# Four heads' shift rows transposed together at the end of the preceding unit, window values produced token-major, and two reorderings on VectorE, in a sparse attention and expert kernel

## What is computed

```python
s_b   = einsum('bhtd,bhnd->bhtn', q, k_c) / scale          # 32 compressed blocks of 16 tokens
out_c = softmax(where(c_ok, s_b, NEG)) @ v_c
_, top_idx = top_k(logits_c, 4)                            # four blocks per token
out_s = softmax over the 64 tokens of the chosen blocks    # selected branch
out_l = softmax over the last 33 tokens                    # window branch
out   = (g0 * out_c + g1 * out_s + g2 * out_l) @ Wo
```

## Time and profile before

| | |
|---|---|
| median of 3 runs | 1492.84 us |
| the profiled execution: its time, its span | 1490.08 us, 1488.3 us |
| busy: PE, DVE, ACT, POOL | 1399.5, 1148.8, 927.1, 946.8 us |
| mean DMA traffic | 76 GB/s |

### The profile page before, as it was taken

How to read it: one execution, slowest core, us unless ns; L and a number is a source line. 1 busy time by engine, 2 the same in 40 slices (tenths; PEclk the granted TensorE clock), 3 DMA queues, 4 the chain that set the end, 5 groups by cost and what they waited for, 6 DMA issues and landing times. The chain is left out here.

```text
span 1488.3 us, 43616 instructions
## 1 busy us (share of the span) xinstructions
PE 1399.5 (94%) x14864; PEld 1041.1 (70%) x14960; DVE 1148.8 (77%) x4512; ACT 927.1 (62%) x1684; POOL 946.8 (64%) x877
## 2 busy tenths in 40 slices
PE   6899569999999999999999999999999999999978
PEld 4566437777777777777777777777777777777757
DVE  5444378888888888888888888888888888888712
ACT  3776436666666666666666666666666666666641
POOL 4655357777777766666666666666676666666720
PEclk8999969999999999999999999999999999999989
DMA  6556842211112222222212222122222222222027
GB/s 187 202 192 213 269 82 54 52 44 48 46 47 51 52 52 52 52 50 47 47 47 47 50 52 47 48 52 52 52 52 52 52 52 52 66 52 53 9 83 250
DMA packets 217149, 113.76 MB, mean 76 GB/s; under 512 B 128872, under 2 KB 211224, under 8 KB 217112
## 3 DMA queue, kind: packets, MB, share of 16 engines
q1 hardware_dynamic: 216304, 112.88, 27.9%
q10 hardware_dynamic: 808, 0.42, 0.2%
HBM read 73.08 MB, written 40.16 MB: 76 GB/s over the span
## 5 line engine op out<-in xcount | busy, mean ns | idle before, releaser
L1394 DVE TENSOR_REDUCE bmax<-q_bank 128x32 f32<-128x512 f32 (+3 forms) x512 | 221.2, 487 | 34.4 <-PE q_bank L1635 34.2
L1149 POOL TENSOR_TENSOR sumxy<-xy 128x1024 f32<-128x1024 f32 x128 | 246.1, 1942 | 0.0
L1241 ACT ACTIVATE pts<-k_bank 128x512 f32<-128x512 f32 (+2 forms) x384 | 177.4, 490 | 42.2 <-PE k_bank L1670 41.4
L1115 POOL TENSOR_TENSOR pad<-pad 128x1 f32<-128x1 f32 x32 | 6.2, 193 | 287.4 <-DVE top L1413 287.4
L1495 DVE SCALAR_TENSOR_TENSOR mw<-sumxy,c,ex 128x1024 f32<-128x1024 f32 x128 | 162.0, 1287 | 13.4 <-ACT ex L1259 9.6
L1617 PE MATMUL f_bank<-xt,wfu 128*128 128x128 f32 x1024 | 162.4, 281 | 0.0
L1635 PE MATMUL q_bank<-ko,qo 96*128 96x512 bf16 (+3 forms) x512 | 142.6, 306 | 16.9 <-DVE bmax L1394 16.7
L1175 POOL TENSOR_TENSOR cw<-cw,mw 128x1024 f32<-128x1024 f32 x64 | 150.9, 2358 | 11.5 <-ACT mw L1265 8.9
L1617 PE MATMUL f_bank<-xt,wfg 128*128 128x128 f32 x1024 | 150.3, 279 | 0.0
L1617 PEld LDWEIGHTS f_bank<-xt,wfu 128*128 128x128 f32 x1024 | 139.4, 191 | 11.5
L1318 ACT ACTIVATE oT<-k_bank 128x512 f32<-128x512 f32 x64 | 38.2, 597 | 173.8 <-PE k_bank L1685 129.3
(11 more groups left out here) (211 smaller groups left out, 3307.8 us busy)
## 6 DMA issues: line engine op xcount, KB each, us to landing
qo<-s_qs SPq DMA_DIRECT2D x192, 64.0 KB, 2.2
ko<-s_ks SPq DMA_DIRECT2D x186, 64.0 KB, 2.2
s_qs<-parts SPq DMA_DIRECT2D x8, 768.0 KB, 4.7
s_ks<-parts SPq DMA_DIRECT2D x8, 768.0 KB, 6.3
s_v<-vo SPq DMA_DIRECT2D x8, 544.0 KB, 3.0
vv<-s_v SPq DMA_DIRECT2D x32, 136.0 KB, 2.3
vw<-s_v SPq DMA_DIRECT2D x64, 68.0 KB, 2.5
xin<-in_L_attn_x_dram SPq DMA_DIRECT2D x8, 512.0 KB, 7.1
```

Source lines behind the costliest of these rows:

```text
L1149: done("sum_done", g_.tensor_tensor(sumxy[:, h, :, :], xy[:, 0, h, 0:XK, None].broadcast_to([P, XK, KEYS]), xy[:, 1, h, None, :].broadcast ...
L1241: last = s.activation(pts[:, h, OFFS[j]:OFFS[j] + n], bank[:, 0:n], ACT.Exp)
L1394: last = v.tensor_reduce(bmax[:, i, h, 0:n], Q.bank(job)[:, o:o + n * BLK].rearrange("p (n j) -> p n j", j=BLK), AX.X, ALU.max)
```

## The change

- **Layout of `qo` and `ko`.** All 128 rows are used by every product. For head `h`, rows 32h to 32h+31 hold the shifts (`qo`) or the one-hot map (`ko`), and the parts lie in the three other quarters. `queries` and `window` multiply over 128 rows, so the shift rows of `qo` must be zero then: four DMAs a unit copy a zero tile from DRAM. `load_parts` has 36 DMAs in place of 12. The one-hot rows are filled once, by DMA from ACT's queue.
- **`head_shifts`.** One job `a` of 4 matmuls with 128 columns each turns all four heads; it stands on PE at the end of the step before, ahead of the second half of `experts_down`. ACT copies it in four pieces at the end of that step, after `window_exp`.
- **`local_values`** multiplies the other way round, so that tokens are on the partitions; it has two halves, around the last part of `mlp_down`, behind `window`. The copy by ACT, the transposes `tl` and their job are gone; `normalize(t, 1)` reads `vl`.
- **`unselected`** stands ahead of `key_marks` on DVE; `normalize(t, 1)` behind `selected_max`; the mask passes of experts 0 and 1 (`expert(n, 0)`, `expert(n, 1)`) at the end of the step before, ahead of `normalize(t, 0)`.
- The last stage finds the first batch's `yr` loaded, and waits for the second batch's `yr` apart from `ar`.

```diff
-            k_jobs = ["pcT", "co", "a0"]
+            k_jobs = ["pcT", "co"]
             for h in range(HG):
-                k_jobs += [f"s{h}0", f"s{h}1", f"s{h}2"] + [f"a{h + 1}"] * (h < HG - 1) + [("pl0", "pl1", "vl", "tl")[h]]
-            k_jobs += ["vs", "ts"]
+                k_jobs += [f"s{h}0", f"s{h}1", f"s{h}2"] + [f"pl{h}"] * (h < 2)
+            k_jobs += ["vl", "vs", "ts", "a"]
...
+            def part_rows(to, src, which, half):
+                for i, pair in enumerate(PARTS):
+                    lots = [(3, i, i + 1)] + [(i, h0, h1) for h0, h1 in ((0, i), (i + 1, HG)) if h0 < h1]
+                    for quad, h0, h1 in lots:
+                        for n in range(2):
+                            o = 32 * quad + D * n
+                            yield to[o:o + D, half, h0:h1, :], src[pair[n][which]][:, h0:h1, :]
...
                 sp.wait_ge(S["st_at"].sem, 16 * (G + 1))
+                sp.wait_ge(S["st_y"].sem, 16 * (G + 1))
                 sp.dma_start(ar0[:, :, :], s_o[0].rearrange("i p c -> p i c")).then_inc(batch_in[0], 16)
+                sp.dma_start(yr0[:, :, :], s_y[0:G].rearrange("i p c -> p i c")).then_inc(batch_in[0], 16)
...
+                    pairs = [(qo[32 * h:32 * h + 32, half, h, :], s_zero) for h in range(HG)]
+                    pairs += part_rows(qo, q, 0, half)
+                    if keys:
+                        pairs += part_rows(ko, k, 1, half)
...
+                def head_shifts(t):
+                    K.wait_full(act, t, "a")
+                    for h in range(HG):
+                        rows = slice(32 * h, 32 * h + 32)
+                        last = s.activation(qo[rows, t.half, h, :], K.bank("a")[rows, :], ACT.Copy)
+                    K.released("a", last)
...
                         expert(n, 0)
                         expert(n, 1)
                         window_exp(n)
+                        head_shifts(n)
...
-                    expert(t, 0)
-                    expert(t, 1)
                     expert_silu(t, 0)
...
                     expert_sum(t)
                     if n:
+                        unselected(n, now=t)
                         key_marks(n)
...
-                    normalize(t, 1)
                     if n:
                         local_scores(n, now=t)
                         selected_max(n)
+                    normalize(t, 1)
+                    if n:
                         pair_sums(n)
                         cn.end()
+                        expert(n, 0)
+                        expert(n, 1)
                     normalize(t, 0)
...
+                def local_values(t, r):
+                    rows = slice(64 * r, 64 * r + 64)
+                    for k in range(2):
+                        for g in range(T // 32):
+                            i, q = divmod(g, 4)
+                            o = VW * (HG * i + 2 * r + k)
+                            last = mm(bank[32 * q:32 * q + 32, o:o + VW], pT[rows, k, 32 * g:32 * g + 32],
+                                      vw[rows, t.half, g, VW * k:VW * k + VW], start=True, stop=True, skip_group_check=True)
...
+                def head_shifts(t):
+                    need(pe, "shift_lo", t)
+                    need(pe, "shift_top", t)
+                    K.wait_free(pe, t, "a")
                     for i in range(TT):
-                        last = mm(K.bank(f"a{h}")[SP3:P, P * i:P * i + P], shift_s[:, i, h, :], identb[:, :],
-                                  start=True, stop=True)
+                        last = mm(K.bank("a")[:, P * i:P * i + P], shift_s[:, i, :, :].rearrange("p h n -> p (h n)"),
+                                  identb[:, :], start=True, stop=True)
...
                     if n:
                         window(n, 0)
                         window(n, 1)
+                    local_values(t, 0)
+                    mlp_down(t, 3)
+                    local_values(t, 1)
                     selected_values(t)
                     transposed_weights(t)
                     experts_down(t, 0)
-                    token_values(t, 0)
+                    token_values(t)
+                    if n:
+                        head_shifts(n)
                     experts_down(t, 1)
```

More of the change, by code:

```diff
@@ L1030, in load_parts @@
                     q, k = row(qs, b)[g], row(ks, b)[g]
-                    pairs = [(to[D * n:D * n + D, half, :, :], src[r])
-                             for to, src, parts in ((qo, q, Q_ROWS), (ko, k, K_ROWS))[:2 if keys else 1] for n, r in enumerate(parts)]
-                    send(pairs, parts_in[half], N_PARTS if keys else N_PARTS // 2)
+                    pairs = [(qo[32 * h:32 * h + 32, half, h, :], s_zero) for h in range(HG)]
+                    pairs += part_rows(qo, q, 0, half)
+                    if keys:
+                        pairs += part_rows(ko, k, 1, half)
+                    send(pairs, parts_in[half], N_PARTS if keys else N_QUERIES)
                 def load_late(b, g, half):
@@ L1304, in window_exp, with selected_values @@
                     done("wl_exp", s.activation(flat, flat, ACT.Exp))
-                def head_shifts(t, h):
-                    K.wait_full(act, t, f"a{h}")
-                    K.released(f"a{h}", s.activation(qo[SP3:P, t.half, h, :], K.bank(f"a{h}")[SP3:P, :], ACT.Copy))
-                def openings(t):
-                    head_shifts(t, 0)
-                    tanh(t, "g0", hidden(0), "th_done")
-                def branch_values(t, k):
-                    job = ("vs", "vl")[k]
-                    K.wait_full(act, t, job)
-                    K.released(job, s.activation(oT[:, k, :], K.bank(job)[:, :], ACT.Copy))
+                def head_shifts(t):
+                    K.wait_full(act, t, "a")
+                    for h in range(HG):
+                        rows = slice(32 * h, 32 * h + 32)
+                        last = s.activation(qo[rows, t.half, h, :], K.bank("a")[rows, :], ACT.Copy)
+                    K.released("a", last)
+                def selected_values(t):
+                    K.wait_full(act, t, "vs")
+                    K.released("vs", s.activation(oT[:, :], K.bank("vs")[:, :], ACT.Copy))
                 def lead(n):
@@ L1634, in queries @@
                         n = P * (i + 1)
-                        last = mm(bank[:, o:o + n], qo[0:SP3, t.half, h, P * i:P * i + P], ko[0:SP3, t.half, h, 0:n],
+                        last = mm(bank[:, o:o + n], qo[:, t.half, h, P * i:P * i + P], ko[:, t.half, h, 0:n],
                                   start=True, stop=(i > 0))
@@ L1695, in local_ready @@
                         K.wait_read(pe, t, f"pl{k}")
-                def local_values(t):
+                def local_values(t, r):
                     bank = K.bank("vl")
-                    for g in range(T // 32):
-                        for h in range(HG):
-                            rows, k = slice(64 * (h // 2), 64 * (h // 2) + 64), h % 2
-                            last = mm(bank[32 * h:32 * h + VW, 32 * g:32 * g + 32], vw[rows, t.half, g, VW * k:VW * k + VW],
-                                      pT[rows, k, 32 * g:32 * g + 32], start=True, stop=True, skip_group_check=True)
-                    K.filled("vl", last)
+                    rows = slice(64 * r, 64 * r + 64)
[5 more added lines that the diff above has]
+                                      vw[rows, t.half, g, VW * k:VW * k + VW], start=True, stop=True, skip_group_check=True)
+                    if r == 0:
+                        done("vl_half", last)
+                    else:
+                        K.filled("vl", last)
                 def local_shares(t, k):
@@ L1818, in step @@
                                 local_shares(t, h)
[L1819 to L1822 removed]
                             if h < 3:
                                 up_rows(t, "ugu"[h], (0, 1, 1)[h], part)
[L1825 removed]
+                            elif part < 3:
                                 mlp_down(t, part)
[L1827 to L1828 removed]
+                            if (h, part) == (3, 2):
+                                local_ready(t)
                             if n and part < 3:
                                 queries(n, h, part)
[L1831 to L1832 removed]
                     if n:
@@ L1847, in build @@
             ar = [ar0] + [sb(f"ar{b}", [P, TT, C]) for b in range(1, B)]
-            yr = [sb(f"yr{b}", [P, TT, C]) for b in range(B)]
+            yr = [yr0] + [sb(f"yr{b}", [P, TT, C]) for b in range(1, B)]
             aT = sb("aT", [P, 2, 2, T])
```

110 lines of the change are left out of this document (52 added, 58 removed).

## The result

The changed kernel takes **1554.87 us** (median of 4 runs, 1552.18 to 1556.18) against 1492.23 us for the kernel before in the same session: a ratio of 1.0416, with an interval of 1.0395 to 1.0437. The forecast was 1558. The profiled execution took 1556.01 us with a span of 1551.9, against 1490.08 and 1488.3; its mean granted clock was 0.976, before 0.981.

The account below looks back on a forecast made before the run. PE, almost without gaps, was taken as the bound, with DVE close behind. Start + 7.2, 30 units x 2.13, last unit - 1.8 and last stage - 2.0 gave + 67.3 on 1490.08: 1557.4, given as 1558 us; range 1514 to 1602.

Parts of the forecast that it names:

- Place and sign: PE's turn ahead of the second half waits for POOL's `shift_s`; a unit grows by 2.13 to 40.50 us; slower 0.89.
- PE up to the turn: PE gains nothing up to `p21`, waiting for DVE, and reaches the new `head_shifts` at 36.31 us from `w0`.
- POOL: POOL's gapless chain from `xy`, started 0.43 us later, ends `shift_s` at 37.11 us, or 38.39 with one collision.
- One collision: In the tail, one moved mask pass goes after `pc` and delays `shift_s` by 1.28 us; forecast case, 0.50.
- Behind it: After `shift_s`, signal 0.05, turn 0.33 and second half 1.73 us follow uncovered: 2.11 us to the next `w0`.
- No collision: POOL's `shift_s` goes before the mask pass: + 0.85 us a unit, 1518 us in all; chance 0.17.
- Two collisions: Mask passes go ahead of both `pc` and `shift_s`: + 3.41 us a unit, 1597 us in all; chance 0.17.
- Faster: DVE's front is not tied to ACT, so PE's whole 1.42 us a unit is gained: 1447 us; chance 0.08.
- SP late: SP's 36 loads land after PE asks for the parts: up to + 50, 1568 to 1610 us; chance 0.05.
- the start: Before unit 0, `w0` must wait for the shifts, ready at 216.47, so unit 1 starts 7.2 us later.
- The end: The last unit has no next, - 1.8 us; the last stage waits less for its first loads, - 2.0 us.

Follow-up runs that it names:

- e4: The changed kernel with the single turn moved from the tail to the unit's own step, behind `w1`: 1508.49 us, ratio 1.0097.
- e10: The changed kernel with the turn in its own step, both moved mask passes and `unsel` back in their old places: 1514.66 us, ratio 1.0151.
- e2: The changed kernel with the two moved mask passes back at the start of DVE's step: 1526.40 us, ratio 1.0233.
- e5: The changed kernel with `unsel` back in its old place, behind POOL's first pair: 1519.33 us, ratio 1.0179.
- e12: The changed kernel with the turn in its own step, third mask pass and first two `ex` earlier, `smax_hi` and `shift_top` later: 1482.66 us, ratio 0.9945.
- e9: The changed kernel with the turn in its own step and both moved mask passes back at the start of DVE's step: 1504.85 us, ratio 1.0094.
- e6: The changed kernel with the turn in its own step and `unsel` back in its old place: 1517.35 us, ratio 1.0170.

## Why the prediction was right

- **Place and sign.** The prediction looked for the end in PE's turn ahead of the second half of the expert product, waiting for POOL's `shift_s`. That is where it is: 1.65 us in nearly each unit. Moving the turn away alone (e4) takes off 46.4 of the 62.6 us.
- **PE up to the turn.** Forecast 36.31 from `w0`, measured 623.12 + 0.43 - 587.08 = 36.47. Both halves of the argument hold: `p21` is later (at 22.35, forecast 22.21), so what PE saves ahead of it becomes waiting. e4 and e10 show it without POOL in play.
- **POOL.** `xy` starts on POOL at 21.18, where the sum had 20.60 + 0.43 = 21.03 (the list at the end of the prediction gives 20.95, which doesn't follow from its own sum). `shift_s` is over at 623.32 + 2.00 - 587.08 = 38.24, forecast 38.39.
- **One collision.** The forecast gave it + 1.28, the length of a mask pass; it measured 2.00 - 1.02 = **0.98**, and e2 shows the same 0.98 in the unit. The error of this term, 0.30 too much, and the 0.15 by which `xy` was later than forecast make the difference between 38.39 and 38.24. The Trainium skill, SBUF — State Buffer, section "Who interferes with whom", has the instruction that is issued first block the other; the trace agrees, in both directions: the waiting pass delays `shift_s` in the changed kernel, and the running `shift_s` delays the pass in e5.
- **Behind it** 2.07 us (625.32 to 627.39), forecast 2.11; the turn took 0.23 instead of 0.33. So the unit is 40.31, forecast 40.50, and the 30 units give + 55.3 (30 x 1.845) instead of + 63.9.
- **The rivals.** "No collision" and its price were right, and e5 and e2 are its cases: 38.97 and 39.33 a unit against 39.22 worked out, 1519 and 1526 against 1518. The margin was a little thinner than forecast: the first `ex` was ready at 35.80 instead of 35.47, and the pass was asked for 0.5 us before the end of `pc`, where the prediction had 0.6. "Two collisions" is the meeting seen in e12; it stretches `pc` by 0.86 and `shift_s` by 0.98, less than the 1.28 each that the prediction took. "Faster" is out: DVE's front was tied to ACT. With the masks gone from it, DVE waits 1.8 us in each unit for the first `tanh` (between 400 and 1200 us: total us, times, longest), and e9 and e4, equal in the loop, show that the masks at its start cost nothing there:

```profile
DVE sw L1523 <- ACT sw L1292: 36.6, 20, 1.8
```

  "SP late" didn't come in the changed kernel (the last load landed 4.5 us after `w0`, and PE asks for the parts at 6.87, so 2.4 us were to spare, forecast 2.6), but did once, near the start, in all experiments except e6.
- **The term that was mis-sized is the start.** The forecast had + 7.2; it measured 267.33 - 254.26 = + 13.1 at unit 1's `w1`. The step said that POOL's `shift_s` ahead of unit 0 would be ready at 216.47 as before, and two things that the change does there were left out. The changed layout gives ACT's queue 20 loads for 6, and ACT copies `sim`, from which `marks` and `xy` come, only behind them. And both `pc` and `shift_s` are stretched there, where before it was `shift_s` alone. The timelines of ACT and of POOL ahead of unit 0 (compare):

```profile
190.80 7.98 ACTq L1252 DMA_DIRECT2D ko<-s_ks  x16
198.91 0.60 ACT L1296 ACTIVATE sim<-f_bank 128x512 f32<-128x512 f32 x1 [26.17 <-issue]
```
```profile
219.06 2.09 POOL L1153 TENSOR_TENSOR pc<-pc,cfac 128x512 f32<-128x512 f32 x1
221.11 1.99 POOL L1158 TENSOR_TENSOR shift_s<-unsel,smax_hi 128x496 bf16<-128x496 bf16 x1
```

  The copy of `sim` was at 193.24 before, so it is 5.7 us later; `shift_s` is now over at 223.1, 6.6 us after the forecast. Of the 5.7 us only 2.5 belong to the longer queue (its first load goes at 188.07, the copy follows 10.84 us behind, before 8.35 us behind the first load at 184.89). The other 3.2 are the later start of the whole stage, and they are not shown to be the change's: in the twelve experiments, which have the changed kernel's code up to there, the first load goes between 184.85 and 190.82. The stretched `pc` adds 1.0.
- **The end** gave back 4.8 us, forecast 3.8. The wait at the last stage's beginning is 4.13 us for `ar`, 1.9 less than the 6.05 for `yr` of the earlier trace rows, forecast 2.0:

```profile
1507.36 4.13 DMA ar<-s_o
```

  The sum: 13.1 + 55.3 - 4.8 = 63.6 us, the difference of the spans (1551.9 - 1488.3), forecast 67.3. The start was 5.9 too small and the units 8.6 too large; that these two errors nearly cancel is luck.

What the change cost, told by the runs: of 62.6 us, some 28 are the collision, some 22 more the turn in the tail without it (e2 against e9, both with the masks back: 1526.4 - 1504.9), and the 13 that are left (e9 against before) are the slower start, with one longer unit near it, and 0.2 us in each other unit. The parts don't add up from their own trials: putting `unsel` back *saves* 35.5 us beside a turn in the tail and *costs* 8.9 us beside a turn in its own step.

## What to carry to other kernels

Before moving a step ahead of work that is ready, find when its last input is ready on every engine, and which instructions of another engine the moved work will meet just then; a margin of half a microsecond decided here over some 35 us (e5). Where parts of a change touch the same meeting, judge them together, since a part that looks bad in the bundle (`unsel`) may be good without its neighbour. And where the bounding engine already waits now and then for a second one, work taken off the first buys only waiting, until the stretch of the second that is waited for becomes shorter, as with the third mask pass.

## What the runs showed of the hardware that was not expected

- Two small instructions of DVE became the ones most stretched. `smax_hi` and the shift's top part took 0.29 and 0.70 us before and 1.05 and 1.88 us in the changed kernel, since DVE came to them while POOL was still in the second `sumxy` pair. The top part by lines, before and in the changed kernel (ns, minimum, median, maximum):

```profile
L1458 DVE TENSOR_TENSOR shift_s<-smax,smax_hi x32: 228/700/704, 213.2 to 1399.7; 128x16 bf16<-128x16 f32 x32
```
```profile
L1475 DVE TENSOR_TENSOR shift_s<-smax,smax_hi x32: 229/1881/1884, 218.9 to 1465.8; 128x16 bf16<-128x16 f32 x32
```

  This operation over 16 elements a partition thus took anything between 0.23 and 1.88 us. In the changed kernel it starts at 619.58, behind the start of POOL's second `sumxy` at 619.47, and ends at 621.46, just behind the end of that one at 621.37; so it is read as waiting for it. POOL's pair was not longer for it (3.76 us).
- The matmuls of the local values took the same time in both forms: 128 records in 1.39 us before, two times 64 in 0.73 each now, with 17 columns streamed and 32 of weights in place of the reverse.
- The single turn of all heads took 0.23 us from start to start, where one head's turn took 0.33, at the same columns streamed and four times the weights' columns.
